# Feed-forward stage in smaller pieces, with the front of each block emitted one block early

## The reference

```
def act_quant(x):                       # per position, over the channels
    scale = 127.0 / clip(max(abs(x)), 1e-5)
    return clip(round(x * scale), -128, 127) / scale

def bit_linear(x, w):  return act_quant(x) @ weight_quant(w).T

h = bit_linear(x, w1)                   # 1024 -> 4096
h = depthwise_conv1d(h, conv_w, conv_b) # 3 taps along the sequence, per channel
h = silu(h)
y = bit_linear(h, w2)                   # 4096 -> 1024
x = layernorm(x + y)
```

## Time and profile before

| | us |
|---|---|
| median of 3 runs | 6126.08 (6110.24 to 6140.30) |
| the profiled execution, its time | 6108.33 |
| its span on core 5, the slowest | 6106.8 |
| spans of the other cores | 6057.9 to 6098.8 |
| the changed stage on core 5 | from 4001.1 to the end |
| PE, DVE, POOL, ACT busy over the span | 2241.6, 1901.3, 1424.7, 855.4 |

### The profile page before, as it was taken

The page is one execution under the profiler, slowest core; times in us unless marked ns, Lnnn a source line. Parts: engine busy times, 40 slices in busy tenths (PEclk is TensorE's granted clock), DMA queues, the critical chain, the costliest instruction groups (busy, mean ns, idle before and its releaser), DMA issues.

```text
span 6106.8 us, 38230 instructions; the slowest of 8 cores (6057.9 to 6106.8 us)
## 1 busy us (share of the span) xinstructions
PE 2241.6 (37%) x11808; PEld 1176.0 (19%) x11808; DVE 1901.3 (31%) x2905; ACT 855.4 (14%) x1551; POOL 1424.7 (23%) x944
## 2 busy tenths in 40 slices
PE   1345431652652653355573000013332333324243
PEld 0111110221221221122241000012222322223132
DVE  0013351332332334322114333223333333243332
ACT  0000031332332222311203000000100000000000
POOL 0000030110110113333324121223323333333433
PEclk8665555776776776577786555556666666666565
DMA  8850006004003001000011533230000000000000
GB/s 144 110 70 1 0 0 178 1 0 110 1 1 103 1 0 56 14 14 14 14 28 44 197 141 119 88 135 0 14 14 0 15 0 14 14 0 14 0 14 7
DMA packets 129333, 258.78 MB, mean 42 GB/s; under 512 B 16457, under 2 KB 79058, under 8 KB 124242
## 3 DMA queue, kind: packets, MB, share of 16 engines
q1 hardware_dynamic: 78802, 202.24, 10.3%
q0 software_dynamic: 50336, 54.11, 6.7%
HBM read 268.22 MB, written 42.21 MB: 51 GB/s over the span
## 4 chain that ended last, share of the span: by engine, by line
PE 34%; DVE 19%; DMA 17%; POOL 15%; issue 7%; ACT 5%; another core or an unknown queue 1%; SPq 1%; DVEq 0%; ACTq 0%; POOLq 0%
PE p4pm L120 8%; PE psm L120 8%; PE p3psv L120 6%; POOL p4tB L136 5%; DMA xkv<-xT 4%; POOL p4tA L136 4%; DMA wqsw2T<-w2T 3%; POOL XB L136 3%; DVE p4tA L136 3%; DVE Y L136 2%; DMA qbuf<-qTw 2%; DVE X L136 2%; DMA wqsw1T<-w1T 2%; DVE p4cmt L148 2%; PE p4pt L123 1%
## 5 line engine op out<-in xcount | busy, mean ns | idle before, releaser
L136 POOL TENSOR_TENSOR Y<-Y,p2asb 128x416 f32<-128x416 f32 x120 | 144.4, 1236 | 1222.3 <-ACT p2bsb L127 1222.3
L120 PE MATMUL p4pm<-p4xq,w1q 128*128 128x260 bf16 x2048 | 261.2, 294 | 398.9 <-DVE p4h L136 316.1
L136 POOL TENSOR_TENSOR p4tB<-p4h,cw 128x2048 f32<-128x2048 bf16 x64 | 295.0, 4610 | 409.9 <-DVE p4h L136 276.2
L120 PE MATMUL p3psv<-XB,w3w 128*128 128x416 bf16 x1280 | 274.7, 384 | 191.1 <-POOL XB L136 190.9
L120 PE MATMUL p4pm<-p4c,w2q 128*128 128x256 bf16 x2048 | 240.6, 283 | 229.4 <-DVE p4c L140 229.4
L120 PEld LDWEIGHTS p4pm<-p4xq,w1q 128*128 128x128 bf16 x2048 | 209.3, 104 | 454.4 <-issue 406.8
L120 PEld LDWEIGHTS p4pm<-p4c,w2q 128*128 128x128 bf16 x2048 | 207.8, 102 | 265.8 <-issue 235.0
L136 POOL TENSOR_TENSOR XB<-X,a3sb 128x416 bf16<-128x416 f32 x160 | 164.8, 1063 | 310.1 <-ACT a3sb L127 310.1
L120 PE MATMUL psm<-VB,w2b 128*128 128x416 bf16 x960 | 213.5, 370 | 14.5 <-ACT t1s L127 14.5
L136 DVE TENSOR_TENSOR p4tA<-p4tA,p4tB 128x2048 f32<-128x2048 f32 x64 | 146.7, 2292 | 230.7 <-POOL p4tB L136 230.5
L123 PE MATMUL p4pt<-idenb,p4c 128*128 128x128 bf16 x512 | 64.7, 305 | 416.3 <-ACT p4c L132 333.2
(11 more groups left out here) (243 smaller groups left out, 4266.2 us busy)
## 6 DMA issues: line engine op xcount, KB each, us to landing
xkv<-xT POOLq DMA_DIRECT2D x32, 1024.0 KB, 16.3
wqsw1T<-w1T SPq DMA_DIRECT2D x16, 2048.0 KB, 9.1
wqsw2T<-w2T SPq DMA_DIRECT2D x64, 512.0 KB, 3.6
qbuf<-qTw SPq DMA_DIRECT2D x96, 256.0 KB, 3.8
sbuf<-sTe SPq DMA_DIRECT2D x96, 256.0 KB, 4.3
xspill<-X SPq DMA_DIRECT2D x2, 8320.0 KB, 27.0
X<-xin SPq DMA_DIRECT2D x1, 8320.0 KB, 49.7
xrb<-xspill SPq DMA_DIRECT2D x5, 1664.0 KB, 9.8
```

The costliest lines, as they stand in the source:

```text
L120: e.matmul(o, l, r, start=s, stop=p), inc, 1)
L136: e.tensor_tensor(o, a, b, p), inc, 1)
```

## The change

- The body of the loop is cut in two functions. `p4_front(t)` holds steps 1 to 3, `p4_back(t)` steps 4 to 7. A new loop emits front(0), front(1), back(0), front(2), back(1) and so on to back(7).
- `xc`, `cmr`, `xq` and `rb1` get two buffers each, chosen by `t % 2`. The front has maxima tiles and a slot of its own (`cmtF`, `tF`).
- To make room, `tA` and `tB` go from 2048 to 512 columns (`tB` has 512 more, which now take the rows and spread factors that `rowq2`, `rb2` and `rb3` held). The convolution runs in 8 pieces of 2 chunks a half, not 2 groups of 8; the second quantisation in 16 pieces, not 4 groups.
- The first quantisation has the one slot `tF` in place of two.
- The mask row is loaded by POOL's queue, with a cast to bf16, and no longer by SP's.
- Waits are added for the shared PSUM and `tB` parts, and the two waits on `p4qa0` and `p4qa1` ahead of each convolution group are gone.

The core of the diff:

```diff
-    QW4 = 8 * OW
-    xc = k.sb("p4x", [128, DCH * TW], F32)
-    cmr = k.sb("p4cm", [1, TW], F32)
-    xq = k.sb("p4xq", [128, DCH * TW], BF16)
+    QW4 = 2 * OW
+    xc = [k.sb(f"p4x{b}", [128, DCH * TW], F32) for b in range(2)]
+    cmr = [k.sb(f"p4cm{b}", [1, TW], BF16) for b in range(2)]
+    xq = [k.sb(f"p4xq{b}", [128, DCH * TW], BF16) for b in range(2)]
+    rb1 = [k.sb(f"p4rb1{b}", [128, 2 * TW], F32) for b in range(2)]
...
+    cmtF = k.sb("p4cmf", [128, 8], F32)
+    tF = k.sb("p4tf", [128, TW], F32)
     tA = k.sb("p4tA", [128, QW4], F32)
-    tB = k.sb("p4tB", [128, QW4], F32)
+    tB = k.sb("p4tB", [128, QW4 + 2 * OW], F32)
...
-    for t in range(JB):
+    def p4_front(t):
+        b = t % 2
         a = t * TW
         k.wait("sync", "p4y", k.val("p4y"))
         k.wait("sync", "p4qm", k.val("p4qm"))
         k.wait("sync", "p4cst", k.val("p4cst"))
...
-        vcm = k.dma("sync", cmr[:], io["cmrow"][0:1, a:a + TW], "p4cmd")
+        k.wait("gpsimd", "p4rowm", k.val("p4rowm"))
+        vcm = k.dma("gpsimd", cmr[b][:], io["cmrow"][0:1, a:a + TW], "p4cmd")
...
         for ch in range(DCH):
-            s = ch % 2
-            sl = tA[:, s * TW:(s + 1) * TW]
-            k.wait("gpsimd", f"p4qa{s}", k.val(f"p4qa{s}"))
+            sl = tF[:]
+            k.wait("gpsimd", "p4qa0", k.val("p4qa0"))
...
+    def p4_back(t):
+        b = t % 2
         k.wait("tensor", "p4oe", k.val("p4oe"))
...
-            for qq in range(2):
-                q0 = qq * 8
+            for qq in range(8):
+                q0 = qq * 2
...
                 for eng in ("vector", "gpsimd"):
                     k.wait(eng, "p4he", vhe)
                     k.wait(eng, "p4cq", k.val("p4cq"))
-                    k.wait(eng, "p4qa0", k.val("p4qa0"))
-                    k.wait(eng, "p4qa1", k.val("p4qa1"))
                     k.wait(eng, "p4yb", k.val("p4yb"))
...
-        for qq in range(4):
-            q0 = qq * 8
+        for qq in range(16):
+            q0 = qq * 2
...
+    for t in range(JB + 1):
+        if t < JB:
+            p4_front(t)
+        if t >= 1:
+            p4_back(t - 1)
```

More of the change, by code:

```diff
@@ L1426, in emit_phase4 @@
         k.wait("vector", "p4cmd", vcm)
-        k.tt("vector", rowq[0:1, 0:TW], rowq[0:1, 0:TW], cmr[0:1, 0:TW], ALU.mult,
-             inc="p4rowm")
+        k.tt("vector", rowq[0:1, 0:TW], rowq[0:1, 0:TW], cmr[b][0:1, 0:TW],
+             ALU.mult, inc="p4rowm")
         k.wait("tensor", "p4rowm", k.val("p4rowm"))
         k.mm(ps_bc[0][:], ones1[:], rowq[0:1, 0:TW], start=True, stop=True)
-        k.mm(ps_bc[1][:], ones1[:], rowq[0:1, TW:2 * TW], start=True, stop=True, inc="p4bc")
+        k.mm(ps_bc[1][:], ones1[:], rowq[0:1, TW:2 * TW], start=True, stop=True,
+             inc="p4bc")
         k.wait("scalar", "p4bc", k.val("p4bc"))
@@ L1441, in emit_phase4 @@
             k.wait("sync", "p4rbe", vrbe)
-            k.dma("sync", io["dbg_rb1"], rb1[:], "p4dbgg")
+            k.dma("sync", io["dbg_rb1"], rb1[b][:], "p4dbgg")
             k.wait("gpsimd", "p4dbgg", k.val("p4dbgg"))
         for ch in range(DCH):
-            s = ch % 2
-            sl = tA[:, s * TW:(s + 1) * TW]
-            k.wait("gpsimd", f"p4qa{s}", k.val(f"p4qa{s}"))
[L1448 to L1452, removed]
-            k.wait("vector", "p4qm", vq1)
[L1454 to L1459, removed]
+            sl = tF[:]
+            k.wait("gpsimd", "p4qa0", k.val("p4qa0"))
+            vq1 = k.tt("gpsimd", sl, xc[b][:, ch * TW:(ch + 1) * TW], rb1[b][:, 0:TW],
+                       ALU.mult, inc="p4qm")
+            k.wait("vector", "p4qm", vq1)
+            vq2 = k.tsc("vector", sl, sl, MAGIC, None, ALU.add, inc="p4qa0")
+            k.wait("vector", "p4qa0", vq2)
+            k.tsc("vector", xq[b][:, ch * TW:(ch + 1) * TW], sl, MAGIC, None,
+                  ALU.subtract, inc="p4qa0")
+        k.wait("tensor", "p4qa0", k.val("p4qa0"))
         if t == 0 and "xq" in P4DBG:
             k.wait("sync", "p4qa0", k.val("p4qa0"))
-            k.wait("sync", "p4qa1", k.val("p4qa1"))
-            k.dma("sync", io["dbg_xq"], xq[:], "p4dbgb")
+            k.dma("sync", io["dbg_xq"], xq[b][:], "p4dbgb")
             k.wait("gpsimd", "p4dbgb", k.val("p4dbgb"))
+    def p4_back(t):
+        b = t % 2
         k.wait("tensor", "p4oe", k.val("p4oe"))
@@ L1473, in emit_phase4 @@
                     k.mm(pm[:], w1q[:, ch * DH + hc * 128: ch * DH + (hc + 1) * 128],
-                         xq[:, ch * TW:(ch + 1) * TW], start=(ch == 0), stop=(ch == DCH - 1),
-                         inc=("p4hm" if ch == DCH - 1 else None))
+                         xq[b][:, ch * TW:(ch + 1) * TW], start=(ch == 0),
+                         stop=(ch == DCH - 1), inc=("p4hm" if ch == DCH - 1 else None))
                 k.wait("vector", "p4hm", k.val("p4hm"))
@@ L1556, in emit_phase4 @@
         k.wait("scalar", "p4bc2", k.val("p4bc2"))
[L1557 to L1558 removed]
+        k.wait("scalar", "p4fm", k.val("p4fm"))
+        k.wait("scalar", "p4fa", k.val("p4fa"))
+        k.cp("scalar", tB[0:1, 2 * OW:3 * OW], ps_bc[0][0:1, 0:OW], inc="p4row2")
+        k.cp("scalar", tB[0:1, 3 * OW:4 * OW], ps_bc[1][0:1, 0:OW], inc="p4row2")
         k.wait("tensor", "p4row2", k.val("p4row2"))
[L1560 to L1561 removed]
+        k.mm(ps_bc[0][:, 0:OW], ones1[:], tB[0:1, 2 * OW:3 * OW], start=True, stop=True)
+        k.mm(ps_bc[1][:, 0:OW], ones1[:], tB[0:1, 3 * OW:4 * OW], start=True, stop=True,
              inc="p4bc2")
@@ L1645, in emit_phase4 @@
             ya = y4n[:, ch * OW:(ch + 1) * OW]
-            vm = k.tt("gpsimd", ya, ya, rb3[:, 0:OW], ALU.mult, inc="p4fm")
+            vm = k.tt("gpsimd", ya, ya, tB[:, 2 * OW:3 * OW], ALU.mult, inc="p4fm")
             k.wait("vector", "p4fm", vm)
-            k.tt("vector", ya, ya, rb3[:, OW:2 * OW], ALU.add, inc="p4fa")
+            k.tt("vector", ya, ya, tB[:, 3 * OW:4 * OW], ALU.add, inc="p4fa")
         vfn = k.val("p4fa")
```

87 lines of the change are left out of this document (44 added, 43 removed).

## The result

The changed kernel takes 6423.58 us (median of 8 runs, 6415.58 to 6441.17), the kernel before, run beside it, 6125.96 (8 runs, 6110.24 to 6140.3). The ratio is 1.0493, with a 95% interval of 1.0474 to 1.0511. It is slower by 298 us where 304 were forecast (6430 less 6126), and its profiled span is 6421.3 us on core 7 against 6106.8. In some executions of every kernel the cores of one die are granted a lower clock and take some per cent longer; the ratios leave such executions out, the medians do not, and where the profiled execution was one of them, a core of the other die is read.

What follows compares the result with a forecast made beforehand. No engine is full; the serial chain of waits inside each stage bounds the kernel. 193 + 86 + 35 - 2 = 312 us on 6108.3 gives 6420; the median runs 18 us higher, so 6430, with 82% for 6350 to 6540.

Steps and rivals of the forecast that it cites:

- What bounds: Last stage, eight blocks: no engine is full; engines take turns, each step starting 0.09 to 0.15 us after the one before.
- Order: Fronts and backs of the last stage: the new order hides no front; only block 1's load comes earlier, 2 us once.
- Convolution: Convolution halves: four serial pieces of 6.53 us, 26.1 instead of 20.4 us a group; 24.1 us a block, +193 us.
- Second quantisation: Second quantisation: 16 serial pieces of 2.39 us, 38.2 instead of 27.5 us; +10.7 us a block, +86 us.
- First quantisation: First quantisation with one slot: 1.67 us a chunk, 13.2 instead of 8.8 us for eight; +4.4 a block, +35 us.
- Mask row: cmrow load moved to POOL's queue: taken at nothing; a slow load would be some 12 us late, 96 over eight blocks.
- Sum: Whole change: 193 + 86 + 35 - 2 = 312 us, on the profiled execution 6420 us.
- 1 (pieces overlap): Convolution and second quantisation: smaller pieces pipeline over POOL, DVE and ACT; -26.7 us a block, 5895 us; chance 3%.
- 2 (front hidden): Fronts of the last stage: hidden after all by the doubled buffers; 242 us less than the sum, 6178 us; chance 3%.
- 3 (POOL's fixed cost): POOL's 512-column instructions: cost per instruction far higher, 184 us more, 6605 us; 8% for anything above the range.
- 4 (clock): PE bursts after longer idle: lower clock throughout adds up to 14.5 us a block, 116 us, 6536 us; chance 2%.
- The port rule: First convolution tap: DVE and GpSimd block each other fully, making it 1.73 us instead of 1.58, sum 19 us larger.

Runs made afterwards that it cites:

- the skewed run: Kernel before with the convolution in pieces of 2 chunks on four slots of tA and tB, steps of three pieces emitted skewed: 6070.76 us, ratio 0.9953.
- the first part: Kernel before with only the convolution cut in 8 pieces of 512 columns a half: 6301.48 us, ratio 1.0325.
- the last run: Changed kernel with the next front mixed into the back, convolution and second quantisation each on DVE alone in two slots: 5445.62 us, ratio 0.8916.

## Why the prediction was right

The forecast was 6430 us and the measured median 6423.58. By its own steps:

- **What bounds.** "So the price of a stage is (work + fixed cost + hand-over) times the number of steps" held: each of the three kinds of piece took the time forecast within 2%, and the growth of each priced stretch, averaged over blocks 1 to 6, came within 0.5 us (the windows above are one block).
- **Order.** That eight fronts and eight backs remain one after the other, with the load exposed behind the store, is what SP's queue shows, and in the run with the old order a block takes as long as with the new one. The early load of block 1 was credited with 2 us. In the trace it is issued 0.12 us after the end of front 0's last POOL multiply (4087.61), and DVE waits for it for 5.1 us instead of the 8.9 from the store to the casts, so it gave some 4. Some 2 more come at the end: no front stands ahead of the last back, and TensorE begins its matmul 8.4 us before the store of the block before it (at 6151.4 and 6159.75). The two make up the 6 us by which the stage is shorter than with the old order; the 2 forecast were too few.
- **Convolution.** 6.53 us a piece forecast, 6.49 measured, and of the steps 1.58 / 1.57, 0.69 / 0.70, 1.04 / 1.04, 0.62 / 0.64. The last gap is 0.19 and not the 0.24 taken. The halves grow by 12.5 and 12.1 us (0.6 of the latter in TensorE's burst) for 12.7 and 11.4; over six blocks it is 13.1 and 11.5. Some luck is in the steps of DVE and ACT: the 256-column row of DVE reads PSUM and the 260-column row of ACT is a cast, unlike the instructions that were to be priced from them.
- **Second quantisation.** 2.39 forecast, 2.36 measured; POOL 1.16 for 1.20, DVE 0.44 for 0.42. +10.4 for +10.7.
- **First quantisation.** 1.67 forecast, 1.68 measured; +3.9 for +4.4 (+4.2 over six blocks). The run of this part alone gave 49 us (32 to 66), an interval that holds the 35; its stage grew by 39.
- **Mask row.** Its cover held: POOL issues it at 4673.98 and DVE reads the row at 4695.87, 12 us after the x load has landed, with no wait for it in the chain.
- **Sum.** +39.2 us a block forecast. From the first store to the last but one a block takes (6159.75 - 4377.87) / 6 = 296.98 us, before, from the first to the last, (6101.03 - 4299.85) / 7 = 257.31: +39.7. That the profiled span came within 1 us of the 6420 worked out for it is partly luck: 11 of its 314 us stand ahead of the stage (its first load is at 4012.1, before at 4001.1), in code that didn't change, and the stage on these two cores grew by 303 for 312.
- **Rivals.** 1 (pieces overlap) fell by the chain: POOL's next tap starts 0.19 us after the SiLU, never before. The Trainium skill, page Perfetto Trace Analysis, section Optimizing Scalar/DVE Operations, which carried this rival, says that breaking instructions up may help where the engines aren't saturated and leave others idle. That was so here, and the pieces cost time. They gained only in the run in which they also had buffers of their own and were emitted interleaved, and there 0.5%. 2 (front hidden) fell by the run with the old order. 3 (POOL's fixed cost) fell by the mean of its 512-column adds, 1037 ns, on the line through the three points. 4 (clock) fell: TensorE idles 52 us ahead of a burst instead of 39.5, and in total its first matmuls took 264.7 us instead of 261.2 and its second 241.8 instead of 240.6. The +2.3 us of the last cut above is mostly scatter between blocks: the second matmul took 29.4 us in one block of before and 31.0 in the next, and over six blocks the cut grew by 0.7.
- **The port rule.** By the rule in full of the Trainium skill, page SBUF — State Buffer, section Who interferes with whom, the first tap was estimated at 1.73 us from the lengths of its steps; my reading of the trace gave 1.58. Measured 1.57. Between free overlap and full exclusion the skewed run also lies near exclusion and not on it.

Of the terms none is off by more than 1 us a block. Parts and whole ran in different sets, in which the kernel before itself had medians of 6095 to 6126 us. By whole times the parts alone add to 198 + 76 + 49 = 323 us, against 298 for the changed kernel in its set and 328 for the one with the old order in the set of the parts. By the stage alone they add to 328, less 17 to 19 for the two waits that the first part keeps, against 314 for the one with the old order: the parts account for the whole. Differences of 20 us between sets are not explained further.

## What to carry to other kernels

Where engines take turns over one buffer, cutting the work in smaller pieces multiplies the fixed costs and hand-overs and overlaps nothing; look for the semaphore on which the next piece's first instruction waits before believing in an overlap. A second buffer and a function called one round earlier hid nothing on engines that execute in order: the instructions of the two rounds had to be mixed, and the load had to stand ahead of the store that waits. And a chain over several engines can be cheaper on one of them, even with eight times the instructions: add up its rows first, to see whether it pays for the slow engine, for the number of passes or for the hand-overs. In a group of 2048 columns the hand-overs were the least.

## What the runs showed of the hardware that was not expected

- DVE and POOL, both on instructions of 512 columns with two inputs, slow each other to about 1.48 us each, from 0.69 and 1.04 alone, when both always have work (the skewed run). A busy time of nearly 100% on both engines hides this; only the mean of one instruction shows it.
- `tensor_scalar` with two per-partition operands on 256 bf16 columns took 334 ns back to back (2.67 us for 8), `scalar_tensor_tensor` 414 ns (6.62 for 16). The mean of one is shown as 405 and 478: neighbours overlap by 64 to 71 ns, so means of one must not be added up for an engine that streams.
- TensorE was granted the full clock for most of a matmul stage in which it worked 1.95 us and waited 1.7 in turn: over the eight blocks of the last run the first matmul had 0.84 to 0.96. In the block shown it fell to the lower level for 7 us; in the next it stayed at 1.00 from 4752.8 to 4798.5.
